# A depthwise 3x3 convolution as banded 64x64 row matrices on image rows

## The chip, the cores and the metric

The kernel runs on one core of a Trainium2 chip. The metric is the device time of one execution in microseconds (us): 211.08 us for the kernel before, the median of 3 runs (210.69 to 211.94). Engines are named as the profile names them: PE (matrix multiply, its weight loads are PEld), DVE (vector), ACT (activation), POOL (general purpose), SP (which only issues transfers here).

## What is computed

The input x is (4, 64, 64, 16), four images of 64 channels, here kept as 64x64 pictures of 16 channels. One block "conv" and one block "ffn" are added to it in turn:

```python
x_dct = DCT over h and w of layernorm(x)                      # (4, 16, 64, 64)
# attention over 8x8 windows of x_dct -> x_low
h1 = gelu(conv1x1(x_dct, c1a_w))
h1 = gelu(conv3x3(h1, c1b_w, pad=1, groups=16))               # depthwise: nine taps for each channel
x_conv = h1 + x_dct
x_high = gelu(conv1x1(x_conv, c2_w)) + x_conv
x_out = coef * x_low + (1 - coef) * x_high + x_dct
x = x + inverse DCT of x_out
# ffn: tokens of 64, layernorm, 8 experts 64 -> 256 -> 64 with gelu,
# softmax router, the two best experts of each token are mixed
x = x + sum over experts of gate * (gelu(xn @ W1 + b1) @ W2 + b2)
```

The change is about the second line, the depthwise convolution, and the 1x1 convolution ahead of it.

## The kernel before

The four images are worked as two pairs (p = 0 and 1; `PAIRS`, `B2` = 2 images each). Each engine has its own function in the block, and in it a list of stages; `in_turn` sorts the stages of both pairs, and the experts' steps `up`, `down`, `gelu` and `add`, by the numbers in the tables `TURN` and `EXPERT_TURN` (L44 to L80). So the order on each engine is written out by hand; semaphores do the rest, and an engine that waits holds up everything behind it in its own list.

On PE pair 0 goes through all of its convolution and attention first, with some stages of pair 1 between (`taps1`, the taps of pair 1, come just ahead of `features0`). Then the experts begin: 64 steps `up` (L723) and 64 steps `down` (L738), 32 units of two steps each, and the remaining stages of pair 1 (`conv_out1` to `gates_to_rows1`) stand between these steps. The first `up` needs the tokens of pair 0: `tokens`, the norm, `high_part` (ACT), `low_part` (POOL), `features` (PE) and `keep_tokens` (ACT).

The stages around the change, in the order in which pair 0 meets them:

- `dct_over_h`, `dct_over_w` (PE, through `transform`, L460), with squares (ACT, L755) and a norm (`norm_columns`, DVE, L994 to L999) between.
- `windows` (PE, L485) transposes; `keep_xd` (ACT, L768) copies the result out, with the window's column and channel on the partitions and (image, row) along the free axis.
- `conv_in` (PE): the first 1x1 convolution as four matmuls of 512 columns with the diagonal-block matrix `enter_bd` (L495), then eight with `conv_bd` (L502) for the two neighbouring columns that belong to other windows. `gelu_in` (ACT, L776 to L780) writes four results into the padded array `h_pad`.
- `places` (L511), `gram_matrices` (L523), `mask_gram` (DVE, L1007), `gram_times_w` (L535), `products` (DVE, L1013), `keep_tk` (ACT, L792), `norms` (PE, L555), `inverse_norms` (DVE: L1025, L1026, the eight operations of `inverse_root` L968 to L975, L1031, L1035), `logits` (PE, L569), `scale_logits` (DVE, L1045): attention.
- `taps` (PE, L582): nine shifted views of `h_pad` times nine diagonal matrices `tap_bd`, summed in PSUM. `gelu_depthwise` (ACT, L798), then `join` (POOL, L919) adds `xd` and gives `x_conv`.
- `norms_of_k` (PE, L593) waits for `dconv_ready`, since it writes into the PSUM slot of the taps; `softmax_in` (DVE, L1054 to L1058), `exponent` (ACT, L808), `softmax_out` (DVE, L1065 to L1067).
- `conv_out` (PE, L603), `gelu_out` (ACT, L803), `high` (POOL, six operations, L926 to L928), `project` (L614), `heads` (L624), `times_wv` (L635), `mask_mix` (DVE, L1076), `low` (PE, L646), `mix_branches` (DVE, L1084, L1086), then back by `to_frequencies` (L655) and two inverse transforms.

On POOL the diagonal-block matrices are built first (L895 to L907). Then comes `weights_of_first` (L942 to L944), which prepares the experts' first weights: it waits for `ffn_in`, that is for both halves of `w1f` and for `w2`, and for `xt_ready`. On DVE `biases` (L1154 to L1158) stands behind `scale_logits0`, and `coefficients` (L986) behind `softmax_in0`. SP issues the loads in this order: the transforms' tables, x (two), the other constants, the first part of `sm`, `w1f` (two halves of 64 partitions), `w1t`, `lnb_rows`, `w2`, the rest of `sm` (`coef`), `c16`.

## Time and profile before

| what | value |
|---|---|
| median of 3 runs | 211.08 us |
| profiled execution, its time | 211.93 us |
| its span, first to last instruction | 209.9 us |
| PE busy in the span | 190.3 us (91%) |
| DVE / ACT / POOL busy | 125.2 / 122.2 / 44.5 us |
| chain that ended last | PE 84%, ACT 6%, DVE 6%, issue 2% |
| first `up` of the experts starts | 79.20 us |
| last `down` ends | 205.9 us |

All starts below are microseconds from the start of the span of this one execution. A busy PE is not PE at its peak: matmuls of several positions of the array run beside each other, and a row's duration is that of the group from its first start to its last end. A row of the timeline gives start, duration, engine, line, operation, output and inputs, shapes, count, and in brackets how long the engine sat idle before it and what ended that.

### The profile page before, as it was taken

To read this page: it belongs to the slowest core of one execution; us is meant where nothing else is said; L and a number is where in the kernel's file an instruction comes from. 1 tells how busy PE (TensorE), PEld (TensorE's weight loads), DVE (VectorE), ACT (ScalarE), POOL (GpSimd) and SP (SyncE) were. 2 spreads that over 40 slices of the span, in tenths; PEclk is the share of its full clock that TensorE was granted. 3 is DMA by queue.
4 is the path that set the end of the run, shared out by engine and by line. 5 is a ranking of instruction groups with operands and counts; after the bars stand their busy time and mean duration, and the time that the engine had idled before them with its cause. 6 is when DMAs were issued, how large, how long until landed. Compare 5 with 4: busy or idle time off the path is not lost.

```text
span 209.9 us, 5812 instructions
## 1 busy us (share of the span) xinstructions
PE 190.3 (91%) x2542; PEld 97.4 (46%) x2542; DVE 125.2 (60%) x237; ACT 122.2 (58%) x206; POOL 44.5 (21%) x49
## 2 busy tenths in 40 slices
PE   7387789969687998999999999999999999999992
PEld 2274753447486332344655444354444453444430
DVE  0645659199498999775554799822533515535354
ACT  2255120386423258988566679678777595584840
POOL 5292960402920061069000050000000000000000
PEclk9969999999999999999999999999999999999998
DMA  6992000000000000294035008153036071091001
GB/s 205 268 279 60 6 3 3 0 5 3 0 8 3 3 0 0 69 243 103 3 94 109 3 2 199 54 141 75 0 100 153 0 178 27 0 210 39 3 0 50
DMA packets 6744, 14.17 MB, mean 68 GB/s; under 512 B 2752, under 2 KB 4288, under 8 KB 5824
## 3 DMA queue, kind: packets, MB, share of 16 engines
q1 hardware_dynamic: 6720, 13.81, 26.8%
q8 instruction: 20, 0.33, 0.7%
q14 instruction: 4, 0.03, 0.1%
HBM read 12.63 MB, written 1.18 MB: 66 GB/s over the span
## 4 chain that ended last, share of the span: by engine, by line
PE 84%; ACT 6%; DVE 6%; issue 2%; POOL 0%; DVEq 0%; POOLq 0%
PE psum L738 27%; PE psum L723 27%; PE psum L582 8%; PE psum L460 4%; PE psum L593 2%; PE psum L453 2%; PE psum L603 2%; PE psum L646 2%; PE psum L535 1%; PE psum L614 1%; PE psum L523 1%; ACT h_pad L776 1%; DVE wide L1013 1%; PE psum L555 1%; PE psum L635 1%
## 5 line engine op out<-in xcount | busy, mean ns | idle before, releaser
L723 PE MATMUL psum<-tok,w1s 128*64 128x512 f16 x512 | 62.6, 380 | 0.6 <-ACT hid L868 0.6
L1173 DVE SCALAR_TENSOR_TENSOR term<-psum,sm,wide 128x512 f32<-128x512 f32 x32 | 24.0, 749 | 47.3 <-PE psum L738 46.3
L868 ACT ACTIVATE hid<-psum,b1p 128x512 f32<-128x512 f32 x64 | 39.5, 692 | 19.2 <-PE psum L723 18.4
L723 PEld LDWEIGHTS psum<-tok,w1s 128*64 128x64 f16 x512 | 28.5, 110 | 41.6 <-issue 14.0
L738 PE MATMUL psum<-hid,w 128*64 128x512 f32 x128 | 31.2, 595 | 0.0
L1178 DVE TENSOR_TENSOR x<-x,term 128x512 f32<-128x512 f32 x32 | 24.5, 764 | 1.1
L868 ACT ACTIVATE w1g<-psum,b1p 128x512 f32<-128x512 f32 x32 | 20.0, 699 | 7.0 <-PE psum L723 7.0
L868 ACT ACTIVATE w1f<-psum,b1p 128x512 f32<-128x512 f32 x32 | 20.1, 702 | 4.9 <-PE psum L723 4.8
L582 PE MATMUL psum<-h_pad,tap_bd 64*64 64x512 f32 x144 | 17.2, 610 | 0.7 <-issue 0.7
L738 PE MATMUL psum<-w1f,w 128*64 128x512 f32 x64 | 16.0, 595 | 0.0
L738 PE MATMUL psum<-w1g,w 128*64 128x512 f32 x64 | 15.9, 595 | 0.0
L738 PEld LDWEIGHTS psum<-hid,w 128*64 128x64 f32 x128 | 8.9, 137 | 10.4 <-issue 6.0
L934 POOL TENSOR_TENSOR place<-place 128x512 f16<-128x512 f32 x4 | 5.0, 1284 | 37.6 <-ACT place L842 37.6
L460 PE MATMUL psum<-c,place 64*64 64x64 f32 x384 | 8.2, 236 | 5.2 <-DVE place L999 4.3
L582 PEld LDWEIGHTS psum<-h_pad,tap_bd 64*64 64x64 f32 x144 | 5.7, 133 | 10.5 <-issue 10.5
L460 PEld LDWEIGHTS psum<-c,place 64*64 64x64 f32 x384 | 7.4, 149 | 6.5 <-DVE place L999 4.5
L798 ACT ACTIVATE place<-psum 128x512 f32<-128x512 f32 x4 | 2.2, 594 | 13.5 <-PE psum L582 13.5
L926 POOL TENSOR_TENSOR place<-place 128x512 f32<-128x512 f32 x4 | 5.7, 1418 | 20.3 <-ACT place L803 20.3
L994 DVE TENSOR_REDUCE st<-place 128x8 f32<-128x512 f32 x4 | 2.6, 683 | 9.9 <-ACT place L755 9.9
L919 POOL TENSOR_TENSOR place<-place 128x1024 f32<-128x1024 f32 x2 | 4.9, 2429 | 11.9 <-ACT place L798 11.9
L738 PEld LDWEIGHTS psum<-w1g,w 128*64 128x64 f32 x64 | 4.4, 137 | 5.8 <-issue 3.7
L738 PEld LDWEIGHTS psum<-w1f,w 128*64 128x64 f32 x64 | 4.4, 137 | 5.5 <-issue 3.6
(141 smaller groups left out, 247.0 us busy)
## 6 DMA issues: line engine op xcount, KB each, us to landing
wide<-gate_store SPq DMA_DIRECT2D x14, 512.0 KB, 6.4
xs<-in_x SPq DMA_DIRECT2D x2, 512.0 KB, 4.1
w1f<-in_W SPq DMA_DIRECT2D x2, 512.0 KB, 9.0
block_out<-x SPq DMA_DIRECT2D x4, 256.0 KB, 6.4
wide<-gate_store SPq DMA_DIRECT2D x2, 384.0 KB, 5.2
hid<-in_W1T SPq DMA_DIRECT2D x1, 512.0 KB, 9.4
w<-in_W SPq DMA_DIRECT2D x1, 512.0 KB, 11.5
c<-const SPq DMA_DIRECT2D x1, 310.0 KB, 6.2
```

Of the source, the lines that this page charges most:

```text
L453: pe.matmul(where, still[:, 0:P], still[:, 0:where.shape[1]], start=True, stop=True)
L460: mm = pe.matmul(quarter(p, j)[rows_of(side), half, n, :], data[rows_of(half), side, 4 * j + n, :], table[rows_of(half), :], start=True, s ...
L582: mm = pe.matmul(bank(slot(p, 0), b)[rows_of(crossed(half, b)), :], tap_bd[rows_of(half), tap, :], shifted(p, b, tap)[rows_of(half)], star ...
L593: mm = pe.matmul(bank(slot(p, 0), j)[rows_of(half), :], half_mask[rows_of(half), :], bank(spread_k[p], j)[rows_of(half), :], start=True, s ...
L723: mm = pe.matmul(h_bank(n)[side * H:(side + 1) * H, :], w1s[:, part, e, k * P + side * H:k * P + (side + 1) * H], tok[:, pair, half, b, :] ...
L738: mm = pe.matmul(y_bank(u)[b * H:(b + 1) * H, :], w2[:, e * KT + k, :], hid_of[u % KEPT][:, B2 * k + b, :], start=k == 0, stop=k == KT - 1)
L868: act.activation(hid_of[u % KEPT][:, B2 * k + b, :], h_bank(n), ACT.Gelu, bias=b1p[:, e * KT + k:e * KT + k + 1]).then_inc(gelu_ready, 1)
L919: pool.tensor_tensor(x_conv[p], x_conv[p], xd[p], ALU.add).then_inc(xconv_ready, 1)
L926: link(pool.tensor_tensor(bank(h2[p], b), bank(h2[p], b), bank(x_conv[p], b), ALU.add))
L934: pool.tensor_tensor(part_of(p, 1, j), split(bank(xc[p], j), H), part_of(p, 0, j), ALU.subtract).then_inc(parts_ready, 1)
L1173: dve.scalar_tensor_tensor(term[:, u % 2, :], y_bank(u), b2t[:, e:e + 1], gate_b[part][:, e % (E // 2), :], ALU.add, ALU.mult).then_inc(te ...
L1178: dve.tensor_tensor(x1p, x1p, term[:, u % 2, :], ALU.add).then_inc(add_done, 1)
```

## The change

- The first convolution now turns the layout as it multiplies: `conv_in` takes slices of a second, unpermuted copy of the windows (`xk`, by the new ACT stage `keep_xk`) as the stationary side and the matrix `enter_bd` as the moving side, 32 matmuls of 64 columns. The result has (image, image row of the window grid) on the partitions and row-in-window, channel, window column along the free axis, and goes through `gelu_in` (now two activations) into `padded`.
- The halo of the depthwise convolution is now two small POOL copies (`wrap`) within `padded`.
- `taps`: for each channel and each of three column offsets one 64x64 banded matrix (three taps along the rows) times 64 columns: 16 channels x 3 x 2 images = 96 matmuls a pair. The bands come from the host (`tap_bands`, 64 x 3072 numbers, loaded twice, once for each half of the partitions).
- `returns` (new, PE): 64 matmuls a pair, with the convolved data as 32-column stationary slices and an identity of 64 columns moving, put the result back on (channel, window column) partitions. `join` moves from POOL to DVE and adds `xd` straight from PSUM.
- The diagonal-block matrices come from the host within `sm`, and POOL builds none. `norms_of_k`, `project` and `conv_out` change PSUM slots, and so what they wait for.
- `hold_clock(12)` (twelve matmuls on zeros) after `dct_over_h0`.
- The loads are issued in another order: bands (two) and the rest of `sm` ahead of `w1f`, `w1t`, `lnb_rows` and `w2`.
- All orders are written anew. Those that matter below (before the experts): PE `dct_over_h0 dct_over_h1 dct_over_w0 windows0 conv_in0 places0 gram_matrices0 dct_over_w1 gram_times_w0 windows1 norms0 logits0 taps0 conv_in1 returns0 norms_of_k0 places1 gram_matrices1 gram_times_w1 conv_out0 project0 heads0 times_wv0 norms1 low0 logits1 to_frequencies0 ... tokens0 taps1 returns1 features0 norms_of_k1`; DVE `... norm_columns1 coefficients mask_gram0 products0 inverse_norms0 scale_logits0 join0 softmax_in0 mask_gram1 softmax_out0 products1 biases mask_mix0 mix_branches0 ...`; POOL `wrap0 weights_of_first high0 wrap1 low_part0`. In `EXPERT_TURN` the steps of unit 12 to the first of unit 15 now stand in one run of seven `up`; the longest run before is six.

```diff
 TURN = {
...
+    "taps": (12, 30), "returns": (14, 31), "norms_of_k": (15, 33), "conv_out": (19, 44), "project": (20, 46),
...
+    "products": (4, 11), "inverse_norms": (5, 15), "scale_logits": (6, 17), "join": (7, 21),
+    "softmax_in": (8, 22), "softmax_out": (10, 23), "biases": (12, 12), "mask_mix": (13, 26),
...
+    "keep_tokens": (24, 54), "tanh_gap": (25, 56), "keep_gates": (28, 60), "wrap": (0, 3),
+    "weights_of_first": (1, 1), "high": (2, 5), "low_part": (4, 6),
 }
...
+def tap_bands(a):
+    taps = a["L0_conv_c1b_w"].reshape(C, 3, 3)
+    out = np.zeros((H, C, 3, H), np.float32)
+    for di in range(3):
+        for row in range(max(0, 1 - di), min(H, H + 1 - di)):
+            out[row + di - 1, :, :, row] = taps[:, di, :]
+    return out.reshape(H, C * 3 * H)
...
-            sp.dma_start(sm[:, 0:COEF], small[:, 0:COEF]).then_inc(weights_in, 16)
+            sp.dma_start(sm[:, 0:LATER], small[:, 0:LATER]).then_inc(weights_in, 16)
+            for half in range(2):
+                sp.dma_start(bands[rows_of(half), :], bands_of).then_inc(bands_in, 16)
+            sp.dma_start(sm[:, LATER:SMALL_N], small[:, LATER:SMALL_N]).then_inc(later_in, 16)
             w1v = W1.rearrange("e d n -> d e n")
             for half in range(2):
                 sp.dma_start(w1f[half * H:(half + 1) * H], w1v).then_inc(ffn_in, 16)
...
-            sp.dma_start(sm[:, COEF:SMALL_N], small[:, COEF:SMALL_N]).then_inc(coef_in, 16)
...
                     transform(p, j, in_chunks(xs[:, p, :]), dct_h).then_inc(dct_h_done, 1)
+                if p == 0:
+                    hold_clock(12, bank(slot(1, 1), 0))
...
             def conv_in(p):
+                pe.wait_ge(weights_in, 16)
                 pe.wait_ge(xd_ready, 2 * (p + 1))
+                pe.wait_ge(xk_ready, 2 * (p + 1))
+                for k in range(K):
+                    for wh in range(2):
+                        for b in range(B2):
+                            mm = pe.matmul(bank(slot(p, 0), wh)[rows_of(b), k * H:(k + 1) * H],
+                                           xk[p][rows_of(wh), (k * B2 + b) * H:(k * B2 + b + 1) * H], enter_bd[rows_of(wh), :],
+                                           start=True, stop=True)
+                mm.then_inc(c1a_done, 1)
...
-                pe.wait_ge(bd_ready, 1)
-                for tap in range(9):
-                    for b in range(B2):
-                        for half in range(2):
-                            mm = pe.matmul(bank(slot(p, 0), b)[rows_of(crossed(half, b)), :], tap_bd[rows_of(half), tap, :],
-                                           shifted(p, b, tap)[rows_of(half)], start=tap == 0, stop=tap == 8)
+                pe.wait_ge(halo_ready, 2 * (p + 1))
+                pe.wait_ge(bands_in, 16 * B2)
+                for c in range(CP):
+                    for dj in range(3):
+                        for x in range(2):
+                            for b in range(B2):
+                                mm = pe.matmul(bank(slot(p, 0), b)[rows_of(x), c * H:(c + 1) * H],
+                                               band(x * CP + c, dj)[rows_of(b), :],
+                                               padded[rows_of(b), p, x * CP + c, dj:dj + K, :].rearrange("p k w -> p (k w)"),
+                                               start=dj == 0, stop=dj == 2)
+                mm.then_inc(taps_done, 1)
+
+            def returns(p):
+                for b in range(B2):
+                    pe.wait_ge(dconv_ready, 2 * p + b + 1)
+                    for k in range(K):
+                        for wh in range(2):
+                            for x in range(2):
+                                at = b * CHUNK + (k * 2 + wh) * H // 2
+                                mm = pe.matmul(bank(slot(p, 0), b)[wh * H + x * H // 2:wh * H + (x + 1) * H // 2, k * H:(k + 1) * H],
+                                               by_channel[p][rows_of(x), at:at + H // 2], ident[rows_of(x), rows_of(x)],
+                                               start=True, stop=True)
+                    mm.then_inc(returns_done, 1)
 
             def norms_of_k(p):
                 pe.wait_ge(spread_ready, p + 1)
-                pe.wait_ge(dconv_ready, 2 * (p + 1))
+                pe.wait_ge(scaled_ready, p + 1)
...
+            def keep_xk(p):
+                for j in range(2):
+                    act.wait_ge(xd_done, 2 * p + j + 1)
+                    act.copy(bank(xk[p], j), bank(slot(p, 0), j)).then_inc(xk_ready, 1)
...
-            def join(p):
-                pool.wait_ge(dconv_ready, 2 * (p + 1))
-                pool.tensor_tensor(x_conv[p], x_conv[p], xd[p], ALU.add).then_inc(xconv_ready, 1)
+            def wrap(p):
+                pool.wait_ge(pad_zero, 2)
+                pool.wait_ge(h1_ready, 2 * (p + 1))
+                pool.tensor_copy(padded[:, p, :, 0, 1:WW], padded[:, p, :, K, 0:WW - 1]).then_inc(halo_ready, 1)
+                pool.tensor_copy(padded[:, p, :, K + 1, 0:WW - 1], padded[:, p, :, 1, 1:WW]).then_inc(halo_ready, 1)
...
+                pool.wait_ge(weights_in, 16)
                 pool.wait_ge(ffn_in, 16 * 3)
-                pool.wait_ge(xt_ready, 1)
...
-                dve.wait_ge(coef_in, 16)
+                dve.wait_ge(later_in, 16)
...
+            def join(p):
+                for b in range(B2):
+                    dve.wait_ge(returns_done, 2 * p + b + 1)
+                    dve.tensor_tensor(by_rows(bank(x_conv[p], b)), by_rows(bank(slot(p, 0), b)), image(xd[p], b),
+                                      ALU.add).then_inc(xconv_ready, 1)
```

## Rows read from the trace of the kernel before

**Rows 1.** The page: busy time of each engine, share of the span, instructions.
```profile
PE 190.3 (91%) x2542; PEld 97.4 (46%) x2542; DVE 125.2 (60%) x237; ACT 122.2 (58%) x206; POOL 44.5 (21%) x49
```

**Rows 2.** Busy time by stretch: stretch, length, engines, granted clock, DMA share, GB/s.
```profile
11.00:14.00 3.00, 2.83 (x105) 2.84 (x108) 0.71 (x2) 1.17 (x2) 3.00 (x12) 0.50 1.06 308
14.50:79.10 64.60, 55.15 (x1232) 34.73 (x1228) 48.15 (x96) 26.62 (x48) 24.75 (x17) 1.00 0.05 12
79.10:205.90 126.80, 126.23 (x1116) 56.56 (x1114) 71.13 (x127) 91.33 (x152) 11.70 (x9) 1.00 0.32 75
```

**Rows 3.** The chain that ended last: start, us, what.
```profile
46.45 0.70 DVE wide L1007
60.18 0.70 DVE place L1086
79.20 0.57 PE psum L723 x4
```

**Rows 4.** Timeline of PE: holds, a transform, 64-column groups, taps, `norms_of_k1`, `up`.
```profile
1.31 3.60 PE L453 MATMUL psum<-still 128*128 128x512 f16 x8 [1.31 <-POOL still L881]
11.16 1.99 PE L460 MATMUL psum<-c,place 64*64 64x64 f32 x64 [4.31 <-DVE place L999]
56.39 2.02 PE L646 MATMUL psum<-place,wide 64*64 64x64 f32 x62 [0.81 <-DVE wide L1076]
58.30 2.03 PE L555 MATMUL psum<-wide,c 64*64 64x64 f32 x126
67.74 8.26 PE L582 MATMUL psum<-h_pad,tap_bd 64*64 64x512 f32 x72
77.26 1.93 PE L593 MATMUL psum<-wide,c 64*64 64x512 f32 x8 [0.27 <-ACT place L798]
166.99 5.35 PE L723 MATMUL psum<-tok,w1s 128*64 128x512 f16 x48
```

**Rows 5.** Timeline of DVE: `inverse_norms0`, `scale_logits0`, `biases`, `softmax_in0`, `route0`.
```profile
28.92 0.63 DVE L968 TENSOR_SCALAR root<-root 128x128 int32<-128x128 int32 x1
29.58 0.29 DVE L969 TENSOR_TENSOR root<-root 128x128 f32<-128x128 f32 x1
33.36 1.23 DVE L1045 TENSOR_TENSOR place<-psum,root 128x1024 f32<-128x1024 f32 x1
34.50 1.22 DVE L1154 TENSOR_TENSOR hid<-hid 128x1024 f32<-128x1024 f32 x1
41.71 0.69 DVE L1054 TENSOR_TENSOR place<-place,psum 128x512 f32<-128x512 f32 x1 [4.53 <-PE psum L593]
77.53 2.32 DVE L1122 TENSOR_TENSOR place<-place,c 128x128 f32<-128x128 f32 x1
```

**Rows 6.** Timeline of POOL: `weights_of_first`, the last of `high0`, `low_part0`, `join1`.
```profile
19.73 3.61 POOL L942 TENSOR_TENSOR w1g<-w1f,sm 128x2048 f32<-128x2048 f32 x1 [4.38 <-ACT place L786]
25.37 4.09 POOL L944 TENSOR_TENSOR w1s<-w1g,w1s 128x2048 f16<-128x2048 f32 x1
57.66 1.28 POOL L928 TENSOR_TENSOR place<-place 128x512 f32<-128x512 f32 x1
72.99 2.32 POOL L934 TENSOR_TENSOR place<-place 128x512 f16<-128x512 f32 x2 [14.06 <-ACT place L842]
77.19 2.50 POOL L919 TENSOR_TENSOR place<-place 128x1024 f32<-128x1024 f32 x1 [1.89 <-ACT place L798]
```

**Rows 7.** DMA rate by stretch (columns as in rows 2): x, then a gate load.
```profile
3.00:7.00 4.00, 3.85 (x69) 2.24 (x67) 0.30 (x1) 0.68 (x2) 0.49 (x1) 1.00 1.02 378
91.00:96.50 5.50, 5.50 (x66) 3.25 (x61) 3.74 (x4) 3.92 (x7) 5.34 (x4) 1.00 1.05 227
```

**Rows 8.** The load of `w2`: when SP issues it, and its time to landing.
```profile
5.97 0.44 SPq L397 DMA_DIRECT2D w<-in_W  x1
DMA to landing us min/median/max: 11.5/11.5/11.5
```

**Rows 9.** Timeline of ACT: `keep_xd0`, two copies of 128x512.
```profile
15.18 1.07 ACT L768 COPY place<-psum 128x512 f32<-128x512 f32 x2
```

206 lines of the change are left out of this document (79 added, 127 removed), and 18 rows, old and new, of the table EXPERT_TURN.

## The prediction

> **What bounds the kernel now.** I read the page's busy times first, then the stretches, then the chain, then each engine's timeline around the change. PE is busy 91% of the span [rows 1], but that mean covers two regimes. From 79.1 to 205.9, where the experts run, PE is busy 126.23 of 126.8 us; from 14.5 to 79.1 it is busy 55.15 of 64.6 and waits in turn for ACT and DVE [rows 2]. The change takes nothing out of the first regime: its `up` and `down` steps and pair 1's stages from `conv_out1` on are the same matmuls in another order. So it is worth what it moves of one moment, the first `up`, at 79.20 in the chain [rows 3]; what happens earlier counts only if it reaches that. The profiled execution took 211.93 us (span 209.9); I add my differences to that and carry them to the median, 211.08, which is 0.85 less. A difference under 0.5% (1.05 us) can't be told from none here.
>
> **Taps.** Now 72 instructions of 512 columns in 8.26 us, 115 ns each, so a matmul is two instructions in fp32 (36 matmuls a pair) [rows 4]. The new 96 matmuls are 192 instructions of 64 columns over the four 64x64 positions in turn. `norms` (L555) uses the four positions in the same way: 126 in 2.03 us, 16.1 ns; `low` (L646), with two positions: 62 in 2.02 us, 32.6 ns [rows 4]. At 16.1 ns: 3.1 us, 5.2 less per pair; at 32.6 ns 6.3. I take 3.1, since the order is that of L555.
>
> **Returns.** 64 matmuls, 128 instructions, on positions of 64 rows by 32 columns; no row shows these. Bounds: 16.1 ns (2.1 us) and 65 ns, twice L646, one position at a time (8.3 us). The four used positions are disjoint in output, as in L555, so I take 2.1.
> The taps before are a test of what shares a bank: two row halves write the same bank b side by side and take 115 ns for 512 columns, where L593, with two positions, takes 1.93/8 = 241 ns [rows 4]; so the halves don't exclude each other. The Trainium skill (TensorEngine Tiling (Array Packing), Restrictions and Gotchas) says that different row tiles can't use one PSUM bank at the same time. By that rule `returns`, whose row halves share a bank, would take the pace of two positions, 4.2 us, and the sum below would rise by some 0.8 us; the row of the taps speaks against it, and so do I.
>
> **First convolution, holds, copies.** `conv_in` goes from 24 instructions to 64 of 64 columns (1.0 us at 16.1 ns): no loss. `keep_xk` adds two ACT copies, 1.07 us by L768 [rows 9], on pair 0's path. Against that, PE sat idle 4.31 us before 11.16, the granted clock in 11.0 to 14.0 was 0.50, its lower level (1.2 GHz), and 64 instructions took 1.99 us, 31 ns each [rows 2, 4]; the twelve holds fill this gap. The first eight holds took 450 ns each (3.60 us) [rows 4]; twelve are 5.4 us at that pace, 2.7 at half of it. The bounds for the start of `inverse_norms0` are 1 us earlier and 3 us later than before; I take 0.7 earlier, L968 wanting to start at 28.2. As the next part shows, this costs or gives nothing, because something else decides there.
>
> **What the loads and POOL do.** Ahead of `w2` SP now issues two band loads, 2 x 786 KB, and 0.29 MB more of the rest (`sm` 0.33 more, tables 0.04 less). Before, `w2` landed at 5.97 + 11.5 = 17.5 [rows 8]. The bands' rate is bounded by x's rows (378 GB/s, 128 partitions) and a gate load's (227 GB/s, 64 partitions, pieces of 8 KB) [rows 7]; bands go to 64 partitions in long pieces, so the second is nearest: 1.573/0.227 = 6.9 us, and 0.29/0.378 = 0.8 for the rest. `w2` lands at 25.2 (22.4 by the first rate). What lies ahead of the bands is 1.5 MB, so the bands end near 13 and the rest of `sm` near 15, an estimate by the same two rates; `taps0` (28.7) and `coefficients`, which now stands ahead of `mask_gram0` (20.6) on DVE and waits for the second, have some 5 us of cover. Gone, it would cost `mask_gram0` what the load is late.
> `weights_of_first` waits for `w2`: its three operations took from 19.73 to 25.37 + 4.09 = 29.46, 9.73 us [rows 6]. They now run from 25.2 to about 34.9, beside `inverse_norms0`. The trace shows what that does: L968 took 0.63 and ended at 29.55, with POOL's third operation at 29.46; L1122, an operation of the 0.29 us kind, took 2.32, from 77.53 to 79.85, while POOL's L919 ran from 77.19 to 79.69 [rows 5, 6]. So a DVE operation on SBUF alone stands until POOL's operation ends, and one is let in at each hand-over. After the change L968 goes after POOL's first, L969 after its second, L970 after its third, which these two delay by 0.5: 35.4 instead of 29.9. From there to the end of L1045 it took 34.59 - 29.90 = 4.7, so 40.1; `norms_of_k0` waits for that (`scaled_ready`) and takes 1.93 [rows 4]; `softmax_in0` starts at 42.1, before 41.71: 0.4 later. `taps0`, `conv_in1` and `returns0` (28.7 to about 35.5) and `join0` lie within this; what the taps save for pair 0 is spent there.
> The Trainium skill (SBUF — State Buffer, Who interferes with whom) gives the reason: VectorE and GpSimd share a port pair, held for a whole instruction, and a VectorE operation with two SBUF inputs or in a two-port mode waits. The trace agrees with its 2.32 against 0.29 us; without the rule the sum would be that of the first rival below.
>
> **From softmax_in0 to x_out0.** `mask_gram1` came at 46.45, 4.74 after `softmax_in0` [rows 3, 5]; now 46.85 at most, and `coefficients` no longer stands between. I take 0.2 later. Two things are now in front of `low0` and `mask_mix0`: `norms1` (2.03, L555) on PE and `biases` on DVE (two operations of 1.22, L1154, and a small one), beside POOL's `high0`, whose end (57.66 + 1.28 = 58.94) released `mix_branches0`, which ended at 60.88 [rows 3 to 6]. Each SBUF-only operation of `biases` takes a turn from `high0`: 1.22 + 0.2 = 1.4 later. Bounds 0 and 1.6 (`norms1` on PE: 2.03 less the 0.5 that `mix_branches0` waits for POOL); I take 1.4. So `x_out0` comes 1.6 later.
>
> **The tail to the first up.** Before, `features0` waited for the taps of pair 1, to 76.0, though `low_part0` had ended at 72.99 + 2.32 = 75.31; 1.26 us after 76.0 came `norms_of_k1`, 1.93 long, then the `up` [rows 3, 4, 6]. With 3.1 for the taps, `features0` waits for `low_part0` alone (Gelu of pair 1's taps now precedes `high_part0`: 0.1), and half of it, 0.6, is left after that: 76.0 against 77.26. `returns1` (2.1) lies under `low_part0`. Gain 1.3.
>
> **The experts.** A run of six `up` (48 instructions, 5.35 us) had no wait [rows 4]; one of seven asks ACT for one step more. Between 0 and 1.0; I take 0.3. The other stages change places only.
>
> **Sum.** 1.6 - 1.3 + 0.3 = +0.6: 211.93 becomes 212.5, the median 211.7.
>
> **The rivals.**
> 1. POOL doesn't hold DVE: `w2` lands early, or few operations are held. With `w2` at 22.4 POOL is done at 32.1, `softmax_in0` starts 2.3 sooner than before, and with +1.5 - 1.3 + 0.3 the median is 209.3. With no hold at all L1045 ends at 33.5, `returns0` at 35.4, `norms_of_k0` at 37.3: 4.4 sooner; with +0.8 (`norms1` alone) - 1.3 + 0.3: 206.5. For it: two rates fit; against it: the gate load's rate, and the 2.32.
> 2. Slower: `returns` runs one position at a time, 8.3 us. `returns0` then ends at 41.6 and not 35.5, 1.5 past what POOL hides; `returns1` ends 4.5 after `low_part0`. 211.7 + 6 = 217.7. It decides from about 27 ns for an instruction (128 x 11 ns = 1.4, what `low_part0` hides). Against it: L555.
> 3. Slower: POOL is released later, at 37.5 and not 35.4, by bands at 175 GB/s. Each microsecond that `w2` lands later is one at the end: 213.8.
> 4. It doesn't do what it says: PE loses 2 x 3 us of taps net, but the first `up` is set by DVE and POOL: that is my forecast.
>
> **How the numbers follow.** Forecast 0.50 (own range 209.8 to 213.2: 0.05 faster, 0.32 same, 0.13 slower); rival 1 0.30 (0.29 faster, 0.01 same), rival 2 0.07, rival 3 0.13 (slower). Faster 0.34, same 0.33, slower 0.33. The range leaves out most of rival 2 and the no-hold end of rival 1: 207.0 to 214.5.
>
> **What would show it.** In the changed profile: L942's successor starting near 25 and the first small operations of `inverse_norms0` stretched to 2 to 4 us beside it; `softmax_in0` near 42; `taps` of 3.1 and `returns` of 2.1 us; no PE wait in the run of seven `up`; first `up` near 79.5. Wrong it is if `w2` lands before 23, if DVE's operations keep 0.29 us beside POOL, or if `returns` takes over 3.5 us.

## The result and the profile after

The changed kernel is slower: 219.83 us median (219.15 to 222.05, four runs) against 210.88 (210.68 to 211.94) for the kernel before beside it, ratio 1.042, 95% interval 1.037 to 1.047. Executions over 1.5% above the fastest of the same kernel are left out of the ratios and intervals, so that a ratio can differ from that of the medians. The forecast was 211.7 with a range of 207.0 to 214.5. The profiled execution took 219.51 us with a span of 217.7.

The experts' stretch did not move. By stretch (length, busy time of PE, its weight loads, DVE, ACT and POOL, granted clock, DMA share, GB/s), from the first `up` to the last `down`:

```profile
85.90:212.62 126.72, 126.14 (x1114) 56.87 (x1114) 69.17 (x122) 91.60 (x151) 11.02 (x8) 1.00 0.32 75
```

That is the row of before [rows 2], 6.7 us later. The chain that ended last (start, us, what) shows what released the first `up` there:

```profile
79.84 0.51 ACT place L871
...
80.42 2.45 POOL place L941 x2
...
84.03 1.86 PE psum L620 x8
85.90 0.57 PE psum L750 x4
```

So of the 7.8 us that the span grew, 6.7 lie ahead of the first `up` [rows 3]; the last 1.1 come between DVE's last operation (207.4 before, 214.1 after) and the end, where the final store lands. From the issue of that store to the end of the span every run below that is built on the changed kernel takes 3.5 to 3.6 us, and every one built on the kernel before 2.4 to 2.5 (but for the streams, which go on behind it). So this 1.1 us, 0.5%, belongs to the changed kernel whatever else is edited, and no run says why.

Ahead of the first `up`, PE is slower in a way that no row of before has in this size: it stands and the profile shows nothing that it waits for ("issue"). Timeline of PE after (start, us, line, operation, operands, tile, count, idle time before and its releaser); L533 is `gram_matrices`, L546 `gram_times_w`, L595 `taps`, L513 `conv_in`, L609 `returns`, L620 `norms_of_k`, L566 `norms`:

```profile
20.25 1.08 PE L533 MATMUL psum<-place 64*64 64x64 f32 x57 [0.68 <-ACT place L814]
24.37 0.38 PE L533 MATMUL psum<-place 64*64 64x64 f32 x4 [3.03 <-issue]
...
26.34 3.63 PE L546 MATMUL psum<-sm,wide 64*64 64x128 f32 x63
...
31.33 2.10 PE L566 MATMUL psum<-wide,c 64*64 64x64 f32 x128
...
34.12 1.32 PE L595 MATMUL psum<-padded,bands 64*64 64x64 f32 x74
36.43 1.91 PE L595 MATMUL psum<-padded,bands 64*64 64x64 f32 x116 [0.99 <-issue]
...
38.19 0.34 PE L513 MATMUL psum<-sm,wide 64*64 64x64 f32 x8
40.30 1.04 PE L513 MATMUL psum<-sm,wide 64*64 64x64 f32 x54 [1.77 <-issue]
41.27 1.30 PE L609 MATMUL psum<-c,place 64*32 64x64 f32 x74
44.30 0.98 PE L609 MATMUL psum<-c,place 64*32 64x64 f32 x54 [1.73 <-issue]
45.21 1.93 PE L620 MATMUL psum<-wide,c 64*64 64x512 f32 x8
...
76.75 1.96 PE L595 MATMUL psum<-padded,bands 64*64 64x64 f32 x115 [1.32 <-issue]
80.21 1.86 PE L609 MATMUL psum<-c,place 64*32 64x64 f32 x115 [0.39 <-issue]
```

Between the stands the matmuls run at the pace of [rows 4]: 116 in 1.91 us are 16.5 ns each (a matmul in these counts is an instruction of the trace, two for one fp32 matmul). With them, the 384 matmuls of `taps0`, `conv_in1` and `returns0` take from 34.30 to 45.28, 10.98 us, 28.6 ns each. The stands come at a fixed distance: between the one of 0.99 and the one of 1.77 lie 116 + 8 matmuls and two short rows of 2, between that and the one of 1.73 lie 54 + 74. That is 128 each time, and with a weight load for each 256 instructions. In each such piece something small is moved. In half microseconds (columns as above), DMA is at 33 GB/s in these and at 0 in those around them, and again at 41.50:

```profile
34.00:34.50 0.50, 0.50 (x40) 0.50 (x36) 0.50 (x1) 0.00 (x0) 0.50 (x1) 1.00 0.11 33
37.50:38.00 0.50, 0.50 (x48) 0.50 (x42) 0.44 (x2) 0.00 (x0) 0.00 (x0) 1.00 0.11 33
```

A stand ends some 2 to 3 us behind its transfer (36.43 behind the first row, 40.30 behind the second). 33 GB/s in half a microsecond are 16.5 KB. The page's table of DMA queues (packets, MB, share) has a queue called "instruction" whose packets have this size: 0.39 MB in 24. First before, then after:

```profile
q8 instruction: 20, 0.33, 0.7%
```

```profile
q8 instruction: 24, 0.39, 0.7%
```

The Trainium skill (Runtime: NRT & Kernel Launch, Instruction fetch mechanics) says that an engine's program is fetched by DMA in blocks of 16 KiB, 256 instructions, while it runs, and that the cost of crossing a block boundary is mostly hidden. The size and the 256 instructions agree; "mostly hidden" doesn't hold for the boundaries in the short steps above, which cost 0.99 to 3.03 us.

The longest stand, 3.03 us, lies where the loads are. In stretches of 5 us the DMA share was 1.07, and behind the stand the granted clock was 0.50, which is 1.2 GHz, where `gram_times_w0` took 3.63 us; 64 such matmuls at the full clock take 1.98 (52.19 in the same timeline).

```profile
20.00:25.00 5.00, 1.71 (x82) 1.63 (x86) 0.09 (x1) 0.20 (x1) 0.00 (x0) 0.82 1.07 262
25.00:30.00 5.00, 5.00 (x123) 4.67 (x116) 2.43 (x3) 1.57 (x3) 2.32 (x1) 0.50 0.13 26
```

DVE and POOL, timelines (POOL's L949 to L951 are `weights_of_first`; on DVE L975 is the first operation of `inverse_norms0`, L1060 `scale_logits0`, L1015 `join0`, L1069 `softmax_in0`):

```profile
27.68 3.60 POOL L949 TENSOR_TENSOR w1g<-w1f,sm 128x2048 f32<-128x2048 f32 x1 [8.22 <-DMA w<-in_W]
...
33.33 4.08 POOL L951 TENSOR_TENSOR w1s<-w1g,w1s 128x2048 f16<-128x2048 f32 x1
```

```profile
33.89 3.60 DVE L975 TENSOR_SCALAR root<-root 128x128 int32<-128x128 int32 x1
...
41.30 1.23 DVE L1060 TENSOR_TENSOR place<-psum,root 128x1024 f32<-128x1024 f32 x1
...
45.34 0.69 DVE L1015 TENSOR_TENSOR place<-psum,place 128x512 f32<-128x512 f32 x1 [2.21 <-PE psum L609]
47.26 0.69 DVE L1069 TENSOR_TENSOR place<-place,psum 128x512 f32<-128x512 f32 x1 [1.23 <-PE psum L620]
```

The hold of DVE by POOL is there, 3.60 us, but it isn't last: `scale_logits0` ends at 42.5, `returns0` at 45.28, and `norms_of_k0` starts behind `returns0`. `softmax_in0` is 5.55 us later than before [rows 5].

### The profile page after: what moved, and what is told of

Its sections match the earlier page's. It is cut to its first block, busy times and chain, and to the rows that moved or that the text cites. A ratio compares the mean times of both kernels' runs of the same rounds, so it can differ in the third digit from the quotient of the medians.

```text
span 217.7 us, 6974 instructions
## 1 busy us (share of the span) xinstructions
PE 188.4 (87%) x3130; PEld 105.6 (48%) x3130; DVE 128.1 (59%) x241; ACT 124.0 (57%) x206; POOL 33.4 (15%) x30
## 4 chain that ended last, share of the span: by engine, by line
PE 77%; DVE 8%; issue 6%; ACT 5%; POOL 1%; DVEq 0%; POOLq 0%
PE psum L765 26%; PE psum L750 25%; PE psum L595 3%; PE psum L474 3%; PE psum L546 3%; PE psum L566 2%; PE psum L620 2%; PE psum L467 2%; PE psum L630 2%; PE psum L513 1%; PE psum L673 1%; ACT hid L897 1%; PE psum L706 1%; POOL place L941 1%; PE psum L641 1%
## 5 line engine op out<-in xcount | busy, mean ns | idle before, releaser
L897 ACT ACTIVATE hid<-psum,b1p 128x512 f32<-128x512 f32 x64 | 39.6, 687 | 19.2 <-PE psum L750 16.6
L750 PEld LDWEIGHTS psum<-tok,w1s 128*64 128x64 f16 x512 | 28.9, 110 | 41.6 <-issue 16.5
L1193 DVE TENSOR_TENSOR x<-x,term 128x512 f32<-128x512 f32 x32 | 23.7, 741 | 1.1
L765 PE MATMUL psum<-w1g,w 128*64 128x512 f32 x64 | 16.2, 594 | 0.0
L933 POOL TENSOR_TENSOR place<-place 128x512 f32<-128x512 f32 x4 | 5.2, 1302 | 33.2 <-ACT place L832 33.2
L595 PE MATMUL psum<-padded,bands 64*64 64x64 f32 x384 | 6.6, 219 | 2.3 <-issue 2.3
L546 PE MATMUL psum<-sm,wide 64*64 64x128 f32 x128 | 5.8, 345 | 2.1 <-DVE wide L1022 2.1
L467 PE MATMUL psum<-still 128*128 128x512 f16 x20 | 6.4, 480 | 1.3 <-POOL still L910 1.3
L595 PEld LDWEIGHTS psum<-padded,bands 64*64 64x64 f32 x384 | 6.2, 135 | 2.6 <-issue 2.6
L609 PE MATMUL psum<-c,place 64*32 64x64 f32 x256 | 4.6, 217 | 2.8 <-issue 2.1
```

Of the source, the lines that this page charges most:

```text
L467: pe.matmul(where, still[:, 0:P], still[:, 0:where.shape[1]], start=True, stop=True)
L546: mm = pe.matmul(bank(slot(p, odd), swapped)[rows_of(crossed(half, swapped)), q * P:(q + 1) * P], gram[p][rows_of(half), i, :], wqk[rows_o ...
L595: mm = pe.matmul(bank(slot(p, 0), b)[rows_of(x), c * H:(c + 1) * H], band(x * CP + c, dj)[rows_of(b), :], padded[rows_of(b), p, x * CP + c ...
L609: mm = pe.matmul(bank(slot(p, 0), b)[wh * H + x * H // 2:wh * H + (x + 1) * H // 2, k * H:(k + 1) * H], by_channel[p][rows_of(x), at:at + ...
L750: mm = pe.matmul(h_bank(n)[side * H:(side + 1) * H, :], w1s[:, part, e, k * P + side * H:k * P + (side + 1) * H], tok[:, pair, half, b, :] ...
L765: mm = pe.matmul(y_bank(u)[b * H:(b + 1) * H, :], w2[:, e * KT + k, :], hid_of[u % KEPT][:, B2 * k + b, :], start=k == 0, stop=k == KT - 1)
```

## The experiments

The theory from the two traces: short instructions on PE outrun the delivery of PE's program, and the band loads delay that delivery further (and `w2`). The rivals: the prediction's own step, that POOL behind the late `w2` holds DVE; the new order of `norms1` and `biases`; the clock. Each run is compared with the kernel before on the same chip. Line numbers shift with the edits.

**The bands loaded last.** The changed kernel with

```diff
-            for half in range(2):
-                sp.dma_start(bands[rows_of(half), :], bands_of).then_inc(bands_in, 16)
...
             sp.dma_start(w2[:, :, :], W2.rearrange("e (k p) d -> p (e k) d", p=P)).then_inc(ffn_in, 16)
+            for half in range(2):
+                sp.dma_start(bands[rows_of(half), :], bands_of).then_inc(bands_in, 16)
```

> The changed kernel with the two band loads moved behind w1f, w1t, lnb_rows and w2; nothing else. Supply theory: PE runs out of instructions. In the trace of the changed kernel a transfer of 16 KB (256 instructions of 64 bytes) shows in single half-microseconds at 34.0, 37.5, 41.5 and 45.5, and PE stands with nothing to wait for at 35.4, 38.5 and 42.6 (0.99, 1.77, 1.73 us); so taps0, conv_in1 and returns0 end at 45.2 whatever POOL and DVE do, and norms_of_k0 comes right behind them. Port theory (the step of the prediction): L975 is held 3.6 us by weights_of_first, and this sets softmax_in0. With w2 some 7 us earlier (about 20.5) that hold goes. Port theory expects softmax_in0 and the whole time about 3 us earlier (216 to 217). Supply theory expects the hold gone and the time within 1 us of the changed kernel (219 to 220.5).

Measured: 222.14 us, above what either theory expected, but with a ratio of 1.044 (1.037 to 1.050) no different from the changed kernel. `weights_of_first` started at 20.47, the hold was gone (L975 took 0.23 us at 35.53), and nothing was gained: `norms_of_k0` (L620) came at 45.67, after the change 45.21. PE's long stand moved with the transfer:

```profile
23.08 2.37 PE L546 MATMUL psum<-sm,wide 64*64 64x128 f32 x57
29.00 0.70 PE L546 MATMUL psum<-sm,wide 64*64 64x128 f32 x7 [3.55 <-issue]
...
45.67 1.93 PE L620 MATMUL psum<-wide,c 64*64 64x512 f32 x8
```

This stand begins where the loads end: from 25.0 on the DMA share in half microseconds is 0.63, 0.40, 0.42, 0.05, and 0 from 27.0 to 29.0. PE goes on 2 us behind the last of it, as it does behind the small transfers above. That the loads kept PE's piece back is inferred from this; no row shows it. But the prediction's hold of DVE by POOL is not what made the changed kernel slow.

**No band load.** The changed kernel without the two loads; POOL zeroes `bands`, so this convolution gives zeros.

```diff
-            for half in range(2):
-                sp.dma_start(bands[rows_of(half), :], bands_of).then_inc(bands_in, 16)
...
+            pool.memset(bands[:, :], 0.0).then_inc(bands_in, 16 * B2)
```

> The changed kernel without the band loads: POOL fills the bands with zeros instead, so the depthwise convolution gives zeros, all else runs as before. Load theory: the 3.03 us stand of PE at 21.3 to 24.4, in the middle of gram_matrices0, and the low clock after it come from the loads, which keep the DMA engines full to 24.5 while PE's next instructions are fetched over the same engines. Then without 1.57 MB of loads the stand shrinks to 1 us or less, mask_gram0 starts 2 to 3 us earlier, gram_times_w0 runs at 2.0 us and not 3.6, and the hold of L975 goes too: 214 to 216. If the stand is only the pace of PE's instruction supply it stays near 3 us whatever the loads, and the time goes down by 1 us or less.

Measured: 215.47 us, ratio 1.017 (1.009 to 1.025). The longest stand of that stretch shrank from 3.03 to 0.58 us, the others stayed (1.06, 1.77 in `conv_in1`, 1.46):

```profile
24.25 0.45 PE L544 MATMUL psum<-sm,wide 64*64 64x128 f32 x7 [0.58 <-issue]
...
32.00 1.91 PE L593 MATMUL psum<-padded,bands 64*64 64x64 f32 x116 [1.06 <-issue]
...
39.59 0.98 PE L607 MATMUL psum<-c,place 64*32 64x64 f32 x54 [1.46 <-issue]
```

Of the loss of 4.2% some 2.5 go with the transfer; the rest needs no transfer.

**Taps in fp16.** The changed kernel with `bands` and `padded` in fp16, so that a matmul of `taps` is one instruction and not two, and the loads have half the bytes.

```diff
-        bands = sb("bands", [P, C * 3 * H])
+        bands = sb("bands", [P, C * 3 * H], F16)
...
-        padded = sb("padded", [P, PAIRS, C, K + 2, WW])
+        padded = sb("padded", [P, PAIRS, C, K + 2, WW], F16)
```

> The changed kernel with padded and bands in fp16: a matmul of the taps is then one instruction and one weight load and not two of each (96 matmuls a pair instead of 192), and the bands are half as many bytes. Supply theory: 192 instructions fewer a pair are three quarters of a 256-instruction piece, 2.8 us less from taps0 to returns0 (11.2 us now) and 1.5 to 2 us less before features0; with the shorter loads 214 to 217. A theory in which the array's time alone counts (16 ns for a matmul) gives 1.5 us less a pair, and where POOL sets the end, what w2's 3.5 us earlier landing gives (about 3 us).

Measured: 216.3 us, ratio 1.016 (1.009 to 1.023). Half the instructions in this one step and half the bytes take 3.5 us off the changed kernel, with the stand in `gram_matrices0` at 1.90 and others still there. This run doesn't separate instructions, bytes and the array's own time, which all go down.

**The delivery by itself.** The kernel before, with three streams of matmuls at the end of PE's program, waiting for nothing: 256 of the form of `taps`, 128 of the form of `returns`, and 64 of 512 columns; each is two matmul instructions in fp32.

```diff
+            for n in range(64):
+                for x in range(2):
+                    for b in range(B2):
+                        pe.matmul(bank(slot(1, 1), b)[rows_of(x), n % 8 * H:(n % 8 + 1) * H], ident[rows_of(b), rows_of(b)],
+                                  dct_w[rows_of(b), :], start=True, stop=True)
...
+                        pe.matmul(bank(slot(1, 0), 0)[first:first + H // 2, n % 8 * H:(n % 8 + 1) * H],
+                                  dct_w[rows_of(x), 0:H // 2], ident[rows_of(x), rows_of(x)], start=True, stop=True)
...
+                        pe.matmul(bank(slot(0, 1), b)[rows_of(crossed(half, b)), :], ident[rows_of(half), rows_of(half)],
+                                  xs[rows_of(half), 0, 0:CHUNK], start=True, stop=True)
```

> The kernel before with three streams of matmuls behind its last one, on constants and into banks no longer read, so that the supply is measured by itself: 256 matmuls of 64x64x64 in fp32 in the taps' order of positions (1024 instructions with their weight loads), 128 of 64x32 positions in the order of returns (512 instructions), 64 of 64x64 with 512 columns (256 instructions). Supply theory: about 3.75 us for 256 instructions, so 13 to 15 us for the first, 7 to 7.5 for the second, both with stands of 1.5 us or more in them, and the third at the array's pace (128 instructions of 115 ns, 14.7 us) with no stand. If the stands in the changed kernel came from something else (loads, waits, banks), the first takes 8.3 us, 16 ns each, and the second 4.2. If the 64x32 positions don't run beside each other, the second takes 8.3 us or more with no stands.

The whole took 240.94 us. Timeline of PE there; L752 has the form of `taps`, L758 that of `returns`, L763 the 512 columns:

```profile
209.66 2.09 PE L752 MATMUL psum<-c 64*64 64x64 f32 x128 [0.99 <-issue]
213.11 2.09 PE L752 MATMUL psum<-c 64*64 64x64 f32 x128 [1.36 <-issue]
216.56 0.93 PE L752 MATMUL psum<-c 64*64 64x64 f32 x47 [1.36 <-issue]
...
220.29 1.99 PE L758 MATMUL psum<-c 64*32 64x64 f32 x128 [1.52 <-issue]
...
224.82 13.96 PE L763 MATMUL psum<-xs,c 64*64 64x512 f32 x128
```

This is the plainest row of the study. From 209.66 on there are no loads, no waits and no other engine at work, and 128 matmuls (each with its weight load: 256 instructions) run in 2.09 us, and then PE stands 1.36 us, twice in the rows shown: 3.45 us for 256 instructions, 27 ns for a short matmul instead of 16 (2.09 us for 128). With 512 columns, 128 take 13.96 us and PE never stands. The 64x32 form has the same pace, 128 in 1.99 us, so `returns` is not slow by its form.

**Taps in fp16 in the kernel before.** Its 72 instructions of 512 columns become 36.

```diff
-        tap_bd = sb("tap_bd", [P, 9, H])
+        tap_bd = sb("tap_bd", [P, 9, H], F16)
...
-        h_pad = sb("h_pad", [P, PAIRS, B2, K + 2, H + 2])
+        h_pad = sb("h_pad", [P, PAIRS, B2, K + 2, H + 2], F16)
```

> The kernel before, with the padded rows and the tap matrices of its own convolution in fp16: 36 matmuls of 512 columns per pair instead of 72. Supply theory (short instructions outrun the delivery of PE's program; instructions of 512 columns do not): no stand at all is added, the taps of a pair take 2.1 to 4.2 us instead of 8.26, and the run gains about as much on the first pair as lies on the chain: 205 to 208 us. Rival (the first pair's taps are hidden by the work of VectorE and GpSimd ahead of softmax_in0, as the prediction's own rival put it): 210 to 211.5 us.

Measured: 211.11 us, ratio 0.9966 (0.9933 to 0.9999): the rival's range, and not the 205 to 208 of the theory. `taps1` took 2.6 us (66.60 to 69.24) instead of 8.26, and nearly all of the saving was lost: the first `up` came 1.3 earlier. DVE, then PE:

```profile
35.02 2.75 DVE L1154 TENSOR_TENSOR hid<-hid 128x1024 f32<-128x1024 f32 x1
...
39.16 0.68 DVE L1054 TENSOR_TENSOR place<-place,psum 128x512 f32<-128x512 f32 x1
```

```profile
44.41 3.69 PE L535 MATMUL psum<-sm,wide 64*64 64x128 f32 x64 [3.05 <-DVE wide L1007]
...
73.16 0.87 PE L695 MATMUL psum<-c,place 128*128 128x128 f16 x8 [3.92 <-POOL place L934]
```

`softmax_in0` (L1054) stood behind `biases` (L1154 and two more), the first of them beside POOL's `join0` (34.34 to 36.69); PE, with less to do, waited for DVE and POOL, and ran L535 at its lower clock behind the wait.

**All three steps in fp16.** The changed kernel with `taps`, `conv_in` and `returns` in fp16 (with a copy of `enter_bd` and the 16-bit identity).

```diff
+        enter16 = sb("enter16", [P, H], F16)
+        bands = sb("bands", [P, C * 3 * H], F16)
...
-                                           xk[p][rows_of(wh), (k * B2 + b) * H:(k * B2 + b + 1) * H], enter_bd[rows_of(wh), :],
+                                           xk[p][rows_of(wh), (k * B2 + b) * H:(k * B2 + b + 1) * H], enter16[rows_of(wh), :],
...
-                                               by_channel[p][rows_of(x), at:at + H // 2], ident[rows_of(x), rows_of(x)],
+                                               by_channel[p][rows_of(x), at:at + H // 2], ident16[rows_of(x), rows_of(x)],
```

> The changed kernel with the taps, the first convolution and the returns all in fp16, so that each of the three steps has half its instructions and the bands half their bytes. Supply theory: the stands in taps, first convolution and returns mostly go, since half the instructions are to be delivered, about 2 to 3 us below the run with fp16 in the taps alone (216.3): 212 to 215 us. Rival (what is left of the loss is the later order of norms, biases and GpSimd's work, which fp16 does not touch): 216 us as before.

Measured: 214.24 us, ratio 1.011 (1.005 to 1.017). The profiled execution, 216.27 us, was the longest of the four.

**All three in fp16 and no band load.** The same, with `bands` zeroed by POOL, so that this convolution gives zeros.

```diff
-            for half in range(2):
-                sp.dma_start(bands[rows_of(half), :], bands_of).then_inc(bands_in, 16)
...
+            pool.memset(bands[:, :], 0.0).then_inc(bands_in, 16 * B2)
```

> The kernel with taps, first convolution and returns in fp16, with the bands zeroed by GpSimd in place of their load, so that its convolution gives zeros. If the loss is made of two parts, the delivery of short instructions and the transfer of the bands, both are now small and the time is 210 to 212 us, level with before. If a third cause is left (order of the norms and biases, clock), it stays at 213 to 214.5 us.

Measured: 209.53 us, ratio 0.988 (0.984 to 0.991). With half the short instructions and no transfer the loss is gone. Halving them also halves the array's time (at 16 ns each, 3.1 of 6.2 us on pair 0), so this run alone doesn't tell the two apart; the streams do. With the load of 0.79 MB, the held operation of DVE and `norms_of_k0` on PE, then `norms_of_k0` without the load:

```profile
32.02 2.46 DVE L979 TENSOR_SCALAR root<-root 128x128 int32<-128x128 int32 x1
...
39.66 3.68 PE L622 MATMUL psum<-wide,c 64*64 64x512 f32 x8 [1.54 <-DVE place L1064]
```

```profile
34.73 1.93 PE L620 MATMUL psum<-wide,c 64*64 64x512 f32 x8
```

Here, with `returns0` early, the hold of DVE by POOL does come last: with the load, `weights_of_first` ran from 24.68 to 34.39, `norms_of_k0` waited 1.54 us for `scale_logits0` (L1064), and then ran at the lower clock (0.50 from 39.6 to 43.3). So in these traces the transfer shows in three ways: the delivery, the hold, and the clock behind the stands. Half the bytes cost nearly as much here (1.011 against 0.988) as all of them in fp32 (1.042 against 1.017).

**The bands' transfer in the kernel before.** The same two loads, of zeros that nothing uses, ahead of the gate weights.

```diff
+        bands = sb("bands", [P, C * 3 * H])
...
+            for half in range(2):
+                sp.dma_start(bands[rows_of(half), :], bands_of).then_inc(bands_in, 16)
             w1v = W1.rearrange("e d n -> d e n")
```

> The kernel before with the change's two band loads (1.57 MB, of zeros, used by nothing) put ahead of the first gate's weights, as the change has them. Load theory from the other side: w2 lands some 5 us later, GpSimd's three operations for the first gate slip with it and inverse_norms0 is held by 3 to 4 us, but the own convolution's matrices have long instructions and PE stands at most once: 211.5 to 214.5 us. Rival (loads by themselves cost nothing, the loss is all PE's short instructions): 210.5 to 211.5 us.

Measured: 215.88 us (213.45 to 217.4), ratio 1.013 (1.007 to 1.019). The profiled execution was the shortest of the four; in it the first `up` is 1.6 us late, `weights_of_first` runs from 25.39 to 35.1, and PE stands 1.00 us in the first convolution. The transfer costs the kernel before something too: 1.3% by the ratio, 2.1% by the medians (215.88 against 211.41), so that how much less than in the changed kernel isn't settled. The median lies above the 211.5 to 214.5 that was expected.

**The order put back.** The changed kernel with two turns of before: `norms1` behind `low0`, `biases` behind `scale_logits0`.

```diff
-    "gram_matrices": (6, 17), "gram_times_w": (8, 18), "norms": (10, 23), "logits": (11, 25),
+    "gram_matrices": (6, 17), "gram_times_w": (8, 18), "norms": (10, 24.5), "logits": (11, 25),
...
-    "softmax_in": (8, 22), "softmax_out": (10, 23), "biases": (12, 12), "mask_mix": (13, 26),
+    "softmax_in": (8, 22), "softmax_out": (10, 23), "biases": (6.5, 6.5), "mask_mix": (13, 26),
```

> The changed kernel with the norms of the second pair put back behind low_part0 and the biases back behind scale_logits0, nothing else. If that order costs what the prediction took (1.4 us between softmax_in0 and x_out0), x_out0 ends about 1.4 to 2 us earlier and the time is 217.5 to 218.5 us. If PE's delivery sets this stretch too, the same instructions are to be delivered in another order and the time stays at 219 to 220 us.

Measured: 219.34 us, ratio 1.037 (1.033 to 1.042), not to be told from the changed kernel.

```profile
52.65 3.58 PE L546 MATMUL psum<-sm,wide 64*64 64x128 f32 x64 [2.13 <-DVE wide L1022]
...
61.41 1.09 PE L662 MATMUL psum<-wide,sm 64*64 64x256 f32 x16 [0.33 <-ACT wide L849]
63.31 2.02 PE L673 MATMUL psum<-place,wide 64*64 64x64 f32 x62 [0.80 <-DVE wide L1091]
```

`low0` (L673) follows `times_wv0` (L662) after 1.90 us instead of 4.03 (59.35 to 63.38 after the change), so the order itself gave 2.1. In this execution L546 ran at the lower clock behind the same wait of 2.13 (3.58 us, 1.98 after the change), which took 1.6 back, and `norms1` now lies behind `low0`. One profile doesn't show how often the clock falls there; the time says that the order is not where the loss is.

**No added holds.** The changed kernel without

```diff
-                if p == 0:
-                    hold_clock(12, bank(slot(1, 1), 0))
```

> The changed kernel without the 12 added clock-holding matmuls behind the first transform. The prediction took them at nothing, because they lie in a gap of TensorE: 219 to 220.5 us. If they keep the clock up where it matters, the time rises to 221 to 223 us; if they only stand in the way of what follows, it falls to 218 to 219 us.

Measured: 219.53 us, ratio 1.032 (1.026 to 1.039). The median is that of the changed kernel, the ratio is 1% lower with intervals that just overlap: no gain from the twelve holds shows, and a cost of up to 1% isn't ruled out.

**A faster kernel.** The kernel before with fp16 taps and one turn changed.

```diff
-    "scale_logits": (5, 16), "biases": (6, 6), "softmax_in": (7, 20), "coefficients": (8, 8),
+    "scale_logits": (5, 16), "biases": (11.5, 11.5), "softmax_in": (7, 20), "coefficients": (8, 8),
```

> The kernel before with its taps in fp16 and, besides, the biases moved on VectorE from ahead of softmax_in0 to behind products1, where VectorE stood 4.67 us. In the fp16 run the join ended at 36.69 us and softmax_in0 began at 39.16, behind the biases. If VectorE's order is what ate the taps' saving, softmax_in0 begins about 2.4 us earlier and the time is 208 to 209.5 us; if TensorE's lower clock in its longer stands ate it, the time stays at 210.5 to 211.5 us.

Measured: 209.78 us (208.13 to 211.27), ratio 0.989 (0.986 to 0.993). `softmax_in0` starts 2.5 us earlier (39.16 with fp16 taps alone), and `biases` run from 48.53:

```profile
36.68 0.69 DVE L1054 TENSOR_TENSOR place<-place,psum 128x512 f32<-128x512 f32 x1 [1.35 <-PE psum L593]
```

This is faster than the kernel before by 1.1%. Of its 2.5 us only 0.6 reach the first `up` of the profiled execution (77.18, with fp16 taps alone 77.81): PE waits the 3.92 us ahead of `features0`, and then `norms_of_k1` runs at the lower clock:

```profile
71.81 2.11 PE L695 MATMUL psum<-c,place 128*128 128x128 f16 x16 [3.92 <-POOL place L934]
73.85 3.40 PE L593 MATMUL psum<-wide,c 64*64 64x512 f32 x8
```

**Holds in that wait.** The same kernel with

```diff
                 pe.wait_ge(logits_read, p + 1)
+                if p == 0:
+                    hold_clock(16, bank(slot(0, 0), 0))
```

> The kernel before with fp16 taps and the biases behind products1, and besides 16 clock-holding matmuls of 512 columns ahead of features0, where TensorE stood 3.92 us waiting for GpSimd and then ran features0 in 2.11 instead of 1.07 us and norms_of_k1 in 3.40 instead of 1.93. If the lower granted clock behind that stand is what costs those 2.5 us, the first up starts about 2.5 us earlier and the time is 207 to 208 us; if GpSimd or ScalarE ends the path there, the time stays at 209 to 210.5 us.

Measured: 211.02 us, ratio 0.9965 (0.9936 to 0.9995), above both expected ranges.

```profile
70.40 5.30 PE L453 MATMUL psum<-still 128*128 128x512 f16 x16 [2.83 <-DVE place L1111]
75.53 1.06 PE L697 MATMUL psum<-c,place 128*128 128x128 f16 x16
76.52 1.94 PE L593 MATMUL psum<-wide,c 64*64 64x512 f32 x8
```

The holds were put behind the wait for `logits_read`, which DVE gives at 70.4. So they began late, ran 5.30 us, with a granted clock of 0.50 from 71 to 74 and 0.99 from 74 to 75, and pushed `features0` from 71.81 to 75.53. What came behind them did run at the full clock, 1.06 and 1.94 us, which is the 2.5 us that the expectation named. Holds ahead of that wait were not tried.

Put together (first `up` in the profiled execution; ratio to before):

| kernel | short steps | band bytes | first `up`, us | ratio |
|---|---|---|---|---|
| before | none, 512 columns | none | 79.13 | 1 |
| before, bands loaded | none, 512 columns | 1.57 MB | 80.72 | 1.013 |
| changed, no load | fp32 | none | 81.23 | 1.017 |
| changed | fp32 | 1.57 MB | 85.83 | 1.042 |
| changed, taps fp16 | taps fp16, half as many | 0.79 MB | 80.91 | 1.016 |
| changed, all fp16 | fp16, half as many | 0.79 MB | 82.58 | 1.011 |
| changed, all fp16, no load | fp16, half as many | none | 75.43 | 0.988 |

Neither the changed kernel without the transfer (1.7%, of which 0.5 is the late end) nor the transfer in the kernel before (1.3%) gives the 4.2%. Their sum is 3.0%, or 3.8% with the 2.1% of the medians; that the two together cost more than their sum is not shown.

## Why the prediction was wrong

Term by term, predicted and then measured, in us later than before: the start of `softmax_in0` 0.4 and 5.55; from there to the end of `x_out0` 1.2 and 1.05; the tail -1.3 and 0.1; the run of seven `up` 0.3 and 0. The sum is 0.6 and 6.7, and the late end adds 1.1 that no term covers. So the first term failed, at the price of PE's short matmuls and at the effect of the loads on PE, which was put at nothing; the tail failed at that price alone.

*What bounds the kernel.* Right: the experts' stretch is unchanged, and 6.7 of the 7.8 us are what the change moved of the first `up`.

*Taps, returns, first convolution.* This is the step that failed by its price. The prediction put 16.1 ns on every short matmul, from groups of 126 that follow other work [rows 4]. The pace of a matmul was right (16.5 ns for `taps`, 16.2 for `returns`), and so was the choice against 32 ns for `returns`; but the sum of the three terms for pair 0's stretch, 3.1 + 1.0 + 2.1 = 6.2 us, measured 10.98, since 384 short matmuls in a row outrun the delivery, by 4.49 us of stands (0.99, 1.77, 1.73). The price of the streams, 3.45 us for 128 or 27 ns, gives 10.4 for 384. In the prediction's own chain these 4.2 us more would still have been covered: `returns0` would have ended at 39.7 and not 35.5, ahead of the 40.1 that POOL was to set. It took the loads as well, as said next: `taps0` also started 5.4 us later than the 28.7 of the prediction, at 34.1. That makes 45.1 for the end of `returns0`; it measured 45.28, behind the 42.5 of `scale_logits0`. `returns0` itself ran from 41.27 to 45.28, 4.0 us, which the prediction had named as a sign of being wrong (over 3.5). The kernel before has it too, in small: its page puts 2% of the chain on "issue", and PE stands 0.28 us within its `norms0` and 0.66 within its `taps0`. On pair 1 the same term was 4.6 us for `taps1`, not 3.1.

*The rule on banks.* `returns`, whose row halves share a bank, took 16.2 ns for a matmul (115 in 1.86 us), and 15.5 when tried by itself. The rule of the Trainium skill (TensorEngine Tiling (Array Packing), Restrictions and Gotchas) that different row tiles can't use one PSUM bank at the same time doesn't show in it.

*Holds, copies, loads.* `conv_in0` started at 15.56, 0.7 before its old 16.31, as worked out, but `gram_matrices0` at 20.25 (before 20.22): with a granted clock of 0.55 from 16.0 to 19.6, `places0` took 1.97 us instead of 1.09. Then came the term that the sum had at nothing, the step that failed first in time: with the bands and gate weights on the queues, 3.03 us of stand, and `gram_times_w0` at 3.63 instead of 2.08 us at the lower clock. `norms0` started at 31.33 and not 25.85, 5.5 later. The two rows of before:

```profile
22.28 2.08 PE L535 MATMUL psum<-sm,wide 64*64 64x128 f32 x62 [0.90 <-DVE wide L1007]
...
25.85 0.81 PE L555 MATMUL psum<-wide,c 64*64 64x64 f32 x40 [0.23 <-DVE wide L1013]
```

The prediction looked at what the loads do to `w2`, and not at what else comes by DMA: PE's own program.

*POOL and DVE.* The mechanism was right, and later than said: `weights_of_first` ran from 27.68 to 37.41 (predicted 25.2 to 34.9; the third rival, 2.1 later, is nearer). DVE came at 33.89 and not at 28.2, so that one operation was held and not three: L975 stood 3.60 us, until POOL's end. The rule of the Trainium skill (SBUF — State Buffer, Who interferes with whom) that the prediction drew on agrees with that number. Its place in the sum was wrong: without the hold, with the bands last, the time did not fall. `returns0` had become later than `scale_logits0`.

*From softmax_in0 to x_out0.* Predicted 1.2 more, measured 1.05 (5.55 late at the one, 6.6 at the other). The size is right, the cause only in part. The biases stood beside `high0` as said (L1173, 1.13 us for a small operation), but `mask_mix0` had its first half done by 62.6, and `low0` came at 63.38, behind `norms1`, in which PE stood once more:

```profile
63.21 0.35 PE L566 MATMUL psum<-wide,c 64*64 64x64 f32 x9 [1.00 <-issue]
```

With the order back 2.1 us were gained at that place and given back elsewhere, so what the order costs is not settled.

*The tail.* Predicted 1.3 earlier, measured 0.1 later: 18.43 us from `x_out0` to the `up` against 18.32. `taps1` ended at 78.71 with a stand of 1.32 in it; the Gelu waits for it, `high_part0` is queued behind that Gelu on ACT, and `low_part0` on POOL behind `high_part0`: 79.84, 80.42 in the chain above. The prediction put this Gelu's place at 0.1 us because it thought the taps short; a late `taps1` goes straight to the end.

*The run of seven `up`.* Predicted 0.3, measured 0: 56 instructions in 6.21 us without a wait.

*The rivals.* The slower rivals named `returns` one position at a time and a late `w2`. The first didn't happen (16.2 ns); the second did, and taking it away gained nothing, since PE came later. That PE's program is itself delivered was not among the rivals.

*Still open.* How the 4.2% divide exactly between stands, hold and clock: each run that removes one moves the others. How the loads hold PE's program back: the stand shrinks without them, but it also outlasts them. And why the last store of a changed kernel lands 1.1 us later.

## What to carry to other kernels

Count PE's instructions as well as its columns: several hundred short matmuls in a row cost 27 ns each here, where the array ran them at 16. Fewer instructions can then be worth more than fewer columns: the 512-column taps in fp16 with `biases` moved took 0.989 of the time before, the changed kernel in fp16 with its load 1.011. Before adding a load to the start of a kernel, look at what short-instruction steps run under it, since the profile counts the transfers of their program on the same 16 DMA engines, and the longest stand of one stretch was 3.03 us under the loads and 0.58 without the bands. And when PE is freed in a stretch that others set, follow the saving: it can come back as a wait and a lower clock, unless the queue that is now last (here DVE's, with `biases` in it) is put in order too.

## What the runs showed of the hardware that was not expected

- 128 matmuls of 64 columns with their weight loads: 2.09 us running, 1.36 us standing, repeated; with 512 columns no stand in 13.96 us.
- Stands lay 128 matmuls, with their weight loads 256 instructions, apart. One grew to 3.03 us while loads had the DMA engines (share 1.07), with the bands last to 3.55 behind their end, and near that place without the band load it was 0.58.
- One DVE operation of 128x128 elements, usually 0.23 us (the same line at 35.53 with the bands last), stood 3.60 us beside POOL's 4.08.
- 16 clock-holding matmuls started after an idle stretch took 5.30 us, 331 ns each: from 71 to 74, in the middle of them, the granted clock was at its lower level (0.50), and from 74 to 75 it was 0.99.
